# Attention with a full bias and an MXFP4 linear: readers of a PSUM ring moved to ScalarE and GpSimd

## The reference

```python
scores = jnp.einsum('bhid,bhjd->bhij', q, k) * scale
bias = jnp.where(in_band, learnable_bias[:, jnp.clip(diag, 0, MAX_BIAS_LENGTH - 1)], 0.0)
scores = jnp.where(causal[None, None], scores + bias[None], -jnp.inf)
m = jnp.maximum(jnp.max(scores, axis=-1), off)
p = jnp.exp(scores - m[..., None])
denom = jnp.sum(p, axis=-1) + jnp.exp(off - m)
out = jnp.einsum('bhij,bhjd->bhid', p, v) / denom[..., None]
x = _layernorm(x + out.transpose(0, 2, 1, 3).reshape(B, S, Dm) @ Wo.T)
x = _layernorm(x + _L0_ffn_ref(x, weight, bias))
```

## Time and profile before

| | us |
|---|---|
| median of 3 runs | 1797.08 |
| lowest, highest | 1792.5, 1806.55 |
| the profiled execution | 1791.66 |
| its span in the profile | 1789.7 |
| TensorE matmul busy in the span | 1572.6 |
| VectorE busy | 1280.2 |
| ScalarE busy | 868.1 |
| GpSimd busy | 226.5 |

### The profile page before, as it was taken

One profiled execution on the slowest core, in us unless ns is written; L12 is line 12 of the kernel. 1 busy time (PEld: TensorE's weight loads), 2 busy tenths in 40 slices (PEclk: granted clock), 3 DMA queues, 4 the chain that ended last, 5 costly groups with the idle time before them and its releaser, 6 DMA issues.

```text
span 1789.7 us, 58704 instructions
## 1 busy us (share of the span) xinstructions
PE 1572.6 (88%) x22192; PEld 798.9 (45%) x22192; DVE 1280.2 (72%) x3801; ACT 868.1 (49%) x1148; POOL 226.5 (13%) x102
## 2 busy tenths in 40 slices
PE   7999999679998998998988999999999898677763
PEld 3444444214544554554554555455455444333331
DVE  2444544498886786877877788788788762689996
ACT  2333333204654554655655566565556566344432
POOL 4323323310000000000000000000000000244443
PEclk9999999857999998999999999999999999899895
DMA  5444444742453345334433262363253312122211
GB/s 208 142 157 154 141 159 152 176 106 50 88 87 51 72 69 85 68 59 80 74 71 52 58 116 51 52 121 53 51 109 65 50 27 78 36 77 75 70 47 47
DMA packets 124026, 155.88 MB, mean 87 GB/s; under 512 B 15169, under 2 KB 79809, under 8 KB 123489
## 3 DMA queue, kind: packets, MB, share of 16 engines
q1 hardware_dynamic: 123744, 152.11, 36.7%
HBM read 100.78 MB, written 50.50 MB: 85 GB/s over the span
## 4 chain that ended last, share of the span: by engine, by line
PE 56%; issue 19%; DVE 17%; POOL 4%; ACT 2%; DMA 1%; DVEq 1%; SPq 0%; POOLq 0%; ACTq 0%
PE ps L625 13%; PE ps L692 11%; PE ps L671 11%; PE ps L651 11%; PE ps L677 6%; DVE junk L1125 5%; DVE mx L1118 4%; PE ps L784 2%; POOL probs L1004 2%; PE ps L702 1%; POOL probs L1035 1%; DVE mx L1125 1%; DVE stats L1298 1%; DMA attn<-wvT 1%; POOL k_stack L1039 1%
## 5 line engine op out<-in xcount | busy, mean ns | idle before, releaser
L870 ACT ACTIVATE probs<-ps 128x1024 f32<-128x1024 f32 (+3 forms) x768 | 604.6, 813 | 424.4 <-PE ps L677 382.8
L651 PE MATMUL ps<-k_stack,q_stack 96*32 96x384 bf16 (+3 forms) x6144 | 541.9, 343 | 61.6 <-DVE mx L1125 31.1
L1125 DVE CUSTOM_DVE_ANT_0 junk<-ps,bias_q 128x384 bf16<-128x384 f32 (+2 forms) x1024 | 500.1, 502 | 129.2 <-PE ps L651 113.3
L671 PE MATMUL ps<-q_stack,k_stack 99*32 99x512 bf16 (+3 forms) x6144 | 534.3, 335 | 18.8 <-issue 16.5
L1118 DVE TENSOR_REDUCE mx<-ps 128x1 f32<-128x128 f32 (+3 forms) x768 | 362.3, 485 | 60.6 <-PE ps L651 56.2
L677 PE MATMUL ps<-toep,flip 96*32 96x384 bf16 (+2 forms) x5120 | 387.3, 285 | 13.1 <-issue 13.1
L625 PE MATMUL ps<-attn 128*128 128x512 f32 x768 | 332.6, 596 | 10.4 <-DMA attn<-hT 9.7
L692 PE MATMUL ps<-probs,v_sb 128*32 128x512 f32 (+3 forms) x3072 | 328.9, 492 | 3.8 <-issue 3.7
L651 PEld LDWEIGHTS ps<-k_stack,q_stack 96*32 96x32 bf16 x6144 | 181.4, 97 | 291.3 <-DVE mx L1125 102.4
L671 PEld LDWEIGHTS ps<-q_stack,k_stack 99*32 99x32 bf16 x6144 | 178.9, 96 | 146.8 <-issue 77.0
L625 PEld LDWEIGHTS ps<-attn 128*128 128x128 f32 x768 | 146.7, 191 | 195.4 <-issue 195.4
(11 more groups left out here) (86 smaller groups left out, 965.7 us busy)
## 6 DMA issues: line engine op xcount, KB each, us to landing
q_stack<-q_parts SPq DMA_DIRECT2D x192, 128.0 KB, 4.2
v_dram<-v_sb SPq DMA_DIRECT2D x32, 512.0 KB, 2.7
v_sb<-v_dram SPq DMA_DIRECT2D x32, 512.0 KB, 8.9
q_parts<-q_stack SPq DMA_DIRECT2D x96, 128.0 KB, 1.9
k_parts<-k_stack SPq DMA_DIRECT2D x96, 128.0 KB, 2.0
k_stack<-k_parts SPq DMA_DIRECT2D x32, 384.0 KB, 7.1
attn<-hT SPq DMA_DIRECT2D x8, 1024.0 KB, 6.2
k_stack<-k_parts SPq DMA_DIRECT2D x32, 256.0 KB, 7.9
```

The source lines that it names most:

```text
L651: mm = pe.matmul(ps_ring[STRIP * a:STRIP * (a + 1), use.bank, 0:c1 - c0], q_stack[0:STACK, b, hl, i:i + STRIP], k_stack[0:STACK, b, hl, c0 ...
L671: mm = pe.matmul(ps_s[STRIP * a:STRIP * (a + 1), u % 2, hh, 0:w], k_stack[0:ROWS, b, hl, j:j + STRIP], q_stack[0:ROWS, b, hl, i0:i0 + w], ...
L870: act.activation(probs[:, (u // 2) % 3, 2 * pr:2 * pr + 2, 0:w], ps_s[:, pr, :, 0:w], ACT.Exp).then_inc(exp_done, 1)
L1125: ins = dve.tensor_tensor_reduce(out=junk[:, use.bank, 0:c1 - lo], in0=ps_ring[:, use.bank, lo - c0:c1 - c0], in1=bias_q[:, hl, BAND - t0 ...
```

## The change

The reading of the transposed banks is taken from VectorE. ScalarE copies the whole bank of O0 and O1 into a new SBUF tile `o_tok`, and that of M into `shift_T`. The copy alone frees the bank. GpSimd then adds the denominators, multiplies, and splits the shifts, all from SBUF. VectorE keeps the reciprocal, between GpSimd's addition and its multiplication. As the ring now has two readers that may overtake one another, the single count of reads is replaced by one per bank, and `Use` gains `turn`, how often the bank has been used before.

The constants set where each engine does its part: ScalarE copies M after exponential 2 (`MT_COPY`), O1 after exponential 5 (`OT_COPY`), O0 after exponential 14 (`OT_0_COPY`), and VectorE takes the reciprocals after its maxima of unit 7 (`RDEN_LEFT`) and 16 (`RDEN_0`). TensorE's order stays as it was.

```diff
+MT_COPY, OT_COPY, OT_0_COPY = 2, 5, 14
+RDEN_LEFT, RDEN_0 = 7, 16
...
         self.before, self.bank = FIRST_STEPS + g * PER_GROUP + place, (FIRST_STEPS + place) % RING
+        self.turn = (FIRST_STEPS + place) // RING + g * (PER_GROUP // RING)
...
+        o_tok = sb("o_tok", [P, 2, 4, HG, VW])
+        shift_T = sb("shift_T", [HG * NB, P])
...
-        ring_read = sem("ring_read")
+        ring_free = [sem(f"ring_free{i}") for i in range(RING)]
...
             def wait_use(use):
-                if not isinstance(use.before, int) or use.before >= RING:
-                    pe.wait_ge(ring_read, use.before - RING + 1)
+                if not isinstance(use.turn, int) or use.turn:
+                    pe.wait_ge(ring_free[use.bank], use.turn)
...
+            def copy_shift(n, use):
+                act.wait_ge(ring_filled, use.before + 1)
+                if not isinstance(n, int) or n:
+                    act.wait_ge(shift_split, n)
+                act.activation(shift_T[:, :], ps_ring[0:HG * NB, use.bank, 0:P], ACT.Copy)\
+                    .then_inc(ring_free[use.bank], 1)
+            def copy_transposed(g, b, n, c, last):
+                use = Use(g, b, f"O{c}", last)
+                act.wait_ge(ring_filled, use.before + 1)
+                act.wait_ge(attn_ready, FIRST + 2 * (n - 1) + c + 1)
+                act.activation(o_tok[:, c].rearrange("p i h w -> p (i h w)"), ps_ring[:, use.bank, :], ACT.Copy)\
+                    .then_inc(ring_free[use.bank], 1)
...
                         exp_unit(g, b, n, u)
                         if b and u == EVAC_LEFT:
                             copy_out(n - 1, 1, NT)
+                        if b and u == MT_COPY and not (last and b > B - AHEAD):
+                            copy_shift(n + 1, Use(g, b - 1, "M", last))
+                        if b and u == OT_COPY:
+                            copy_transposed(g, b - 1, n - 1, 1, last)
                         if u == EVAC_0:
                             copy_out(n, 0, T_OF_CHUNK[0])
+                        if u == OT_0_COPY:
+                            copy_transposed(g, b, n, 0, last)
...
                     if b == B - 1:
+                        if not last:
+                            copy_shift(n + 2, Use(g, b, "M", last))
                         copy_out(n, 1, NT)
+                        copy_transposed(g, b, n, 1, last)
...
+            def normalise(g, b, n, c, last):
+                use = Use(g, b, f"O{c}", last)
+                f = 2 * n + c
+                pool.wait_ge(ring_free[use.bank], use.turn + 1)
+                pool.wait_ge(e_off_ready, n + 1)
+                pool.tensor_tensor(den[:, c], o_tok[:, c, :, :, D],
+                                   e_off[:, b, :].rearrange("p (h i) -> p i h", h=HG)[:, c * 4:(c + 1) * 4, :],
+                                   ALU.add).then_inc(den_ready, 1)
+                pool.wait_ge(rden_ready, f + 1)
+                dst = attn[:, b * NB + c * 4:b * NB + c * 4 + 4, bass.ds(g * HG * D, HG * D)]
+                pool.tensor_tensor(dst.rearrange("p i (h d) -> p i h d", h=HG), o_tok[:, c, :, :, 0:D],
+                                   rden[:, c].unsqueeze(3).broadcast_to([P, 4, HG, D]),
+                                   ALU.mult).then_inc(attn_ready, 1)
...
-                ins.then_inc(ring_read, 1)
+                ins.then_inc(ring_free[use.bank], 1)
...
+            def reciprocals(n, c):
+                dve.wait_ge(den_ready, FIRST + 2 * n + c + 1)
+                dve.reciprocal(rden[:, c], den[:, c]).then_inc(rden_ready, 1)
...
-                        if b and u == MT_LEFT and not (last and b > B - AHEAD):
-                            next_shifts(g, b - 1, n - 1)
                         if more and u == SPREAD - 1:
                             shifts(ga, n + 2, ba % 2, use_of(NM - 1))
-                        if b and u == OT_LEFT:
-                            normalise(g, b - 1, n - 1, 1, last)
-                        if u == OT_0:
-                            normalise(g, b, n, 0, last)
+                        if b and u == RDEN_LEFT:
+                            reciprocals(n - 1, 1)
+                        if u == RDEN_0:
+                            reciprocals(n, 0)
```

More of the change, by code:

```diff
@@ L158, in first @@
         self.before = n * (NM + 1) + k
-        self.bank = self.before % RING
+        self.turn, self.bank = divmod(self.before, RING)
         return self
+USES_OF_BANK = [len(range(i, ALL_USES, RING)) for i in range(RING)]
 def ahead(g, b, k=AHEAD):
@@ L882, in _ @@
             for n in range(AHEAD):
+                copy_shift(n, Use.first(n, NM))
                 exp_off(n, n)
```

104 lines of the change are left out of this document (56 added, 48 removed).

## The result

| | before | after |
|---|---|---|
| median of 4 runs, us | 1799.76 | 1834.74 |
| lowest, highest | 1792.5, 1806.55 | 1824.1, 1837.02 |
| the profiled execution's span | 1789.7 | 1830.6 |
| TensorE matmul busy in the span | 1572.6 | 1579.2 |
| VectorE busy | 1280.2 | 1222.5 |

After over before is 1.0183, with an interval of 1.0125 to 1.0242: the changed kernel is slower by some 35 us. The forecast was 1837.

What follows compares the result with a forecast made beforehand. TensorE was taken to set attention's pace, level with VectorE in each batch's first part. Longer-held banks +67, VectorE's relief -30, group ends +2 and attention's end +1 gave +40 us: a median of 1837, range 1793 to 1877.

Steps and rivals of the forecast that it cites:

- a bank that is held longer: In attention, TensorE's third maximum after a transpose waits for ScalarE's copy at O0, M and O1: +67 us, bounds 0 to 100.
- the forecast's list of what would be seen: TensorE's waits view: about 30 waits of 1.3 to 1.5 us and 22 of about 0.5 for o_tok, 22 of 0.9 for shift_T.
- VectorE's relief: In each batch's first part, less VectorE work gives back TensorE's idle time ahead of maxima: -30 us, bounds 9 to 36.
- The lower bound of 9: Least return from VectorE's lighter load: the listed 15 us of TensorE waits without the long ones at four group starts.
- The counter per bank: Ahead of TensorE's maxima, a third as many register instructions: worth 0 to 3 us, taken as 0.
- its own signs: Wrong if copies come two maxima ahead, waits for VectorE do not shrink, or issue waits shrink by more than 20 us.
- Group ends: VectorE's last instruction before its loop jump comes some 0.4 us later, exposed in four groups, +2; attention's end, +1.
- Where the work goes: ScalarE gets 47 us and has room; GpSimd gets 4 us or less per batch, and nothing waits for it.
- B: Rival: VectorE sets the pace of each batch's first part, so its removed work shortens the path: -18, 1779 us; chance 0.09.
- D: Rival: GpSimd working beside VectorE holds it up in the full stretch, none of the 30 returns: +100, 1897 us; chance 0.07.
- C: Rival: TensorE's new waits for banks fall into its issue waits, up to 40 of 45 us go: net 0, 1797; chance 0.19.

Runs made afterwards that it cites:

- m_o1_early: The changed kernel with ScalarE copying M after exponential 1 instead of 2 and O1 after 4 instead of 5; 1800.58 us, 1.0020 of before.
- dve_spend: all_early with unused reductions put on VectorE where the removed work had stood; 1776.79 us, 0.9823 of before.
- counters_only: The kernel before with one counter of reads per bank and nothing else, VectorE still reading every bank; 1774.38 us, 0.9840 of before.
- all_early: The changed kernel with all three ScalarE copies (M, O1, O0) one exponential earlier; 1769.16 us, 0.9806 of before.
- counters_parity: counters_only with the count of exponentials split in two by the unit's parity; 1776.08 us, 0.9860 of before.
- exp_parity: all_early with the count of exponentials split in two by the unit's parity; 1766.08 us, 0.9762 of before.

## Why the prediction was right, and where not

**Slower, by a bank that is held longer: right.** The mechanism and its size were as forecast, and TensorE waits at the three places. It stands idle at O0 for 1.31 us in the mean where 1.35 was worked out, at M 0.91 for 0.91, at O1 0.50 for 0.48; 26, 22 and 22 of them for 27, 22 and 22; together 65 us for 67. Undoing the constants takes off 66. That these agree so well is in part luck: O1's wait only stood in for one for VectorE (m_o1_early), so its 11 us are not part of the loss, and fewer issue waits made up for them. The copy took 592 ns for the 602 of the earlier trace rows, that of M 260 for 280. ScalarE's exponential 15 starts 2.35 us after exponential 14 (1132.18 to 1134.53), where two in a row stand 0.95 apart. The waits view shows 1.2, 0.3 and 0.8 and not these, for the reason told above; the forecast's list of what would be seen should have been 0.15 lower in that view.

**VectorE's relief, -30: the step that failed.** The forecast took the short idles ahead of maxima in units 4 to 7 to be VectorE's backlog, 1.0 us per batch, and let the removed work give all of it back. The waits for VectorE in the view are 17 us before and 17 after, and the short ones among them (below 0.8 us) 9.3 and 6.6. By dve_spend three quarters of the load are worth 3 us, by counters_only against all_early all of it is worth 5, both within the measurement; by counters_parity against exp_parity it is 10 by the medians, with 10 us fewer issue waits beside it. The 30 are refuted. The lower bound of 9 is not, by that last pair, but no run shows that the waits for VectorE shrink by its relief. The first 15 us of a batch do not gain by it, although VectorE was busy 14.30 of them, because the wait in the narrow units is not a backlog, as shown under dve_spend: at a lower load VectorE stands idle just before it. In that stretch of the changed kernel it is busy 12.25:

```profile
1073.00:1088.00 15.00, 13.75 (x301) 7.28 (x293) 12.25 (x45) 9.79 (x16) 2.25 (x6) 1.00 0.48 78
```

**The counter per bank, 0 to 3 us, taken as 0: the other step that failed.** It is worth 26 us. The order rows showed the register instructions go, and they were counted as work of some nanoseconds beside matmuls. The 45 us of issue waits were right there to ask what makes them. The forecast called each "one late block", which is what the trace bears out (below), and left them as they were; but a changed stream changes which blocks are late.

So the sum came out right with two wrong terms that nearly cancel. By the forecast: +67 - 30 + 0 + 3 = +40. By the runs: +66 (places) - 5 (relief) - 26 (counters) = +35, a sum that closes by the way its terms are taken, each as the difference of two neighbouring kernels. So the number was right by luck in two of its terms. The forecast's reasons would have said that moving the copies earlier gives 1770, which is right, and that it gives it by relieving VectorE, which is wrong. By its own signs, two of the three on which it would be wrong came true: the waits for VectorE did not shrink, and the issue waits shrank by 21 us, from 49 to 28.

**Group ends, +3**: the four waits for VectorE at group starts are 2.7 long each now, 10.7 together; before they were 2.4 at most, 7.4 for the five above 0.8. Right in size, though the forecast's own lengths (0.60 and 0.48 in place of 0.85) make 0.23 a group and not the 0.4 that it took.

**Where the work goes.** GpSimd is busy 96.8 us in attention (80 to 130 forecast), and TensorE never waits for it. VectorE's reciprocal does, 12 times, 71.2 us in all, up to 14.5 us; before, its addition waited 12 times for the transpose, 48.5 us. Whether that costs anything was not tried. GpSimd's two instructions for O0 and O1:

```profile
L1092 POOL TENSOR_TENSOR den<-o_tok,e_off 128x16 f32<-128x16 f32 x64 | 15.4, 240 | 516.6 <-ACT o_tok L905 516.6
...
L1097 POOL TENSOR_TENSOR attn<-o_tok,rden 128x256 f32 (+1 forms) x64 | 39.6, 619 | 202.8 <-DVE rden L1253 202.8
```

The multiplication took 619 ns for an estimated 480, the addition 240 for at most 480. VectorE lost 55 us for an estimated 74: the removed instructions are 73 us long together, but instructions on it overlap by some 0.08 us, which a sum of lengths counts twice.

**The rivals.** B (VectorE's relief wins, 1779) is refuted: it needs a relief near 57, and that is 5, 10 at most by the medians. D (GpSimd holds VectorE, 1897; with its own 4 less 2.6 us per batch it should have been 1909) is refuted by the length of the reductions, which read PSUM and at most one operand from SBUF:

```profile
L1225 DVE CUSTOM_DVE_ANT_0 junk<-ps,bias_q 128x384 bf16<-128x384 f32 (+2 forms) x1024 | 501.1, 500 | 163.2 <-PE ps L665 146.1
...
L1218 DVE TENSOR_REDUCE mx<-ps 128x1 f32<-128x128 f32 (+3 forms) x768 | 366.2, 488 | 118.2 <-PE ps L665 113.7
```

500 and 488 ns after, 502 and 485 in counters_only, where GpSimd does nothing in attention. Of the 120 reductions of 384 elements at L1218 in attention, 44 ran beside a busy GpSimd for over half their length: 556 ns in the mean, 557 for the other 76. The Trainium skill's rule ("SBUF — State Buffer", Who interferes with whom), that a VectorE instruction with at most one SBUF input doesn't contend with GpSimd, agrees with these rows.

C (the new waits fall into the issue waits, 1797) is half true. The issue waits fell from 49 us to 28, just past the 20 us that the forecast named as the point where it would be wrong. But the time did not go to 1797, and all_early has even fewer, 23, with no waits for copies for them to fall into. So the new waits did not take them in. Nor is the shorter stream alone enough: counters_only and counters_parity, with streams as short or shorter, have 41 and 37 us. The six kernels in which ScalarE copies, without added increments and with the maxima's places as they were, have 20 to 30. What in the move lowers them is open.

**What the issue waits are.** The trace has TensorE's instructions as they are fetched: page section 3 of before lists 179 packets of kind "instruction" on queue 8, 2.93 MB, 16 KB each, for TensorE's 46,658 instructions, so one packet is a block of 256. Three things show that the issue waits are such blocks coming late. First, along a stretch without a jump the waits stand whole multiples of 256 instructions apart: in before the first seven are 6, 5, 6, 4, 7 and 5 blocks apart. Second, all 299 issue waits of the 14 profiles end 1.2 to 2.0 us after a block of queue 8 has landed; a moment picked at random lies so in one case of eight. Third, the trace shows when a block is late. Where the other transfers kept the 16 DMA engines busy for nine tenths or more of the 3 us before the block's transfer began, TensorE waited for 268 of 654 blocks; otherwise for 31 of 1714, and 28 of these 31 stand some 4 us behind TensorE's jump back, two in each profile. The wait of 2.31 us shown at the end of this document is one: the block goes out at 1091.19 with the engines full, lands at 1092.49, and TensorE goes on at 1094.06.

So the issue waits are blocks of instructions that are fetched late, behind a jump or, most of them, while the kernel's own loads fill the DMA engines. That the loads are the cause is read from these counts; no run moved the loads. The Trainium skill ("Runtime: NRT & Kernel Launch", Instruction fetch mechanics) has crossing a block of fetched instructions mostly hidden. The trace agrees for 142 of the 171 blocks in attention of before; the other 29 cost 0.26 to 3.5 us each, 49 us in all.

**What stays open.** 768 increments add three blocks to some 170, which does not make ten more long waits. They also move the end of every block, and with it which ends fall into the bursts of loads. 768 increments cost 37 us spread evenly and some 23 in wide units, 810 register instructions gave back 26, and 290 others gave nothing. Whether the length of the stream costs anything apart from where the block ends fall, no run tells. Nor was it tried to spread the loads, which is the change that these counts ask for.

## What to carry to other kernels

Where an engine with time to spare takes over the read that frees a slot, its place in that engine's queue matters more than the work moved: ask when the bottleneck engine wants the slot again, and put the read ahead of the instruction that waits for that engine's next step. all_early differs from the change by three numbers and is 3.7% faster than it; it and exp_parity, at 0.9806 and 0.9762 of before, are the versions to keep. Before a wait is counted as a loss, look for another that would take its place: O1's did.

Ask what the waits are for which no semaphore is seen, and look at the instruction packets and at the kernel's own loads around them. A counter that needs no new value at each wait was worth more here than 55 us of work taken from a neighbour, but another 290 instructions less were worth nothing: such a gain has to be measured each time, and need not last when the program changes elsewhere.

A time that comes out right does not show that its terms are: two of the four here were wrong. Undo the terms one at a time.

## What the runs showed of the hardware

TensorE can pay for instructions that wait for nothing: 768 counter increments in some 45,900 instructions made attention 37 us longer (1061.8 to 1098.9 us from the first exponential to the last), none of it in the units themselves.

TensorE's instructions come in blocks of 256, and a block whose fetch starts while the DMA engines are full is late in 268 cases of 654, otherwise in 31 of 1714.

The long issue waits are not spread evenly. In before and after alike most stand between unit 12 and unit 16 of a batch, and behind TensorE's jump back; the matmuls behind them run at the lower clock, 1.2 GHz, for a while. Such a stretch of after (batch 18): a wait of 2.31 us at 1094.06, with the DMA engines full before it (the share of 1.12 below), and from 1094 to 1107 a mean clock of 0.74, where 1073 to 1088 has 1.00:

```profile
1094.06 0.34 PE L665 MATMUL ps<-k_stack,q_stack 96*32 96x384 bf16 x1 [2.31 <-issue]
...
1096.34 0.43 PE L691 MATMUL ps<-toep,flip 96*32 96x256 bf16 x4
1096.55 0.53 PE L665 MATMUL ps<-k_stack,q_stack 96*32 96x384 bf16 x4
...
1098.47 0.62 PE L665 MATMUL ps<-k_stack,q_stack 96*32 96x512 bf16 x4 [0.74 <-ACT o_tok L905]
```

```profile
1091.00:1094.00 3.00, 0.75 (x11) 0.09 (x3) 0.35 (x3) 0.83 (x1) 0.00 (x0) 1.00 1.12 214
1094.00:1107.00 13.00, 12.20 (x170) 5.42 (x173) 6.80 (x24) 5.61 (x7) 0.86 (x2) 0.74 0.02 5
```

The same 256 columns start 0.21 apart from the next matmul here and 0.11 in the O0 shown first. The wait for the copy is shorter for it, 0.74 for 1.21, since TensorE comes to the bank later: the slow matmuls hide 0.47 us of a wait, and 13 us at 0.74 cost some 3 (an estimate from these rows).
